# A larger GpSimd descriptor ring, setup weights on row buffers, and exponentials written back into their bank

## The reference

```python
h = _L0_tok_ref(x, ...)                              # embedding, hashed n-gram rows, scan, MLP
h = h + _L0_attn_ref(_layernorm(h, axis=-1), ...)    # windowed attention with shifted keys
h = h + _L0_ffn_ref(_layernorm(h, axis=-1), ...)     # 8 experts, the best one is taken
h = h + _L1_attn_ref(_layernorm(h, axis=-1), ...)    # "diagonal" attention, 8 heads
h = h + _L1_ffn_ref(_layernorm(h, axis=-1), ...)     # product keys, 16 table rows per head, causal attention
```

## Time and profile before

| what | value |
| --- | --- |
| median of 3 runs | 7602.68 us |
| lowest and highest | 7565.14 and 7603.8 us |
| the profiled execution | 7555.76 us |
| its span | 7554.0 us |
| mean granted TensorE clock | 0.655 of full speed |
| PE, DVE, ACT, POOL busy | 47%, 40%, 32%, 60% of the span |

### The profile page before, as it was taken

The page is one execution under the profiler, slowest core; times in us unless marked ns, Lnnn a source line. Parts: engine busy times, 40 slices in busy tenths (PEclk is TensorE's granted clock), DMA queues, the critical chain, the costliest instruction groups (busy, mean ns, idle before and its releaser), DMA issues.

```text
span 7554.0 us, 47644 instructions
## 1 busy us (share of the span) xinstructions
PE 3587.5 (47%) x10858; PEld 1925.2 (25%) x10858; DVE 2987.1 (40%) x10577; ACT 2449.4 (32%) x6449; POOL 4565.1 (60%) x4472
## 2 busy tenths in 40 slices
PE   3569979623334444443444345433543444444334
PEld 1247754211112212221222122211221222122112
DVE  4667744443333333332333333433433333333301
ACT  1247733212333333332333333322332323332222
POOL 4238820046666666666666666766666666666764
PEclk8567866556666666666666666766666666666667
DMA  1000012211112221122122111212121122111221
GB/s 24 13 17 24 23 37 79 71 36 51 49 48 50 54 50 48 49 54 49 47 48 56 47 49 49 55 48 49 48 55 48 48 49 49 48 45 46 48 46 31
DMA packets 228682, 346.51 MB, mean 46 GB/s; under 512 B 111343, under 2 KB 150836, under 8 KB 228416
## 3 DMA queue, kind: packets, MB, share of 16 engines
q0 software_dynamic: 135168, 272.90, 15.0%
q1 hardware_dynamic: 93248, 70.74, 3.0%
HBM read 310.84 MB, written 32.52 MB: 45 GB/s over the span
## 4 chain that ended last, share of the span: by engine, by line
another core or an unknown queue 28%; DVE 24%; issue 22%; PE 5%; ACT 2%; DVEq 0%; ACTq 0%
DVE sq_is_cand L2027 3%; PE sq_ps_v L1764 3%; DVE sq_is_cand L2025 3%; DVE sq_row_f L2029 3%; DVE sq_kv L2075 2%; DVE sq_d_negmax L1934 2%; DVE sq_top_at L1996 1%; ACT sq_rows L1892 1%; DVE sq_c_negmax L2080 1%; DVE sq_sim_rest L1984 1%; DVE sq_top_at L1985 1%; DVE sq_tops L1992 1%; DVE sq_cand_rest L1984 1%; DVE sq_tops L1980 1%
## 5 line engine op out<-in xcount | busy, mean ns | idle before, releaser
L1676 POOL DMA_INDIRECT sq_rows<-in_L_ffn_table,sq_row x4096 | 4005.9, 978 | 2082.2 <-issue 1218.1
L1764 PE MATMUL sq_ps_v<-sq_rows,sq_ident 128*128 128x512 f32 x2048 | 1360.3, 825 | 953.3 <-remote 412.0
L1892 ACT ACTIVATE sq_rows<-sq_rows,sq_weight 128x128 f32<-128x128 f32 x4096 | 1250.7, 397 | 207.3 <-issue 200.2
L1764 PEld LDWEIGHTS sq_ps_v<-sq_rows,sq_ident 128*128 128x128 f32 x2048 | 532.5, 274 | 1648.6 <-issue 802.6
L1843 ACT ACTIVATE sq_prob<-sq_ps_c,sq_c_negmax 128x128 f32<-128x128 f32 (+3 forms) x256 | 135.1, 528 | 1726.6 <-remote 630.6
L1832 ACT ACTIVATE sq_exp_out<-sq_ps_d,sq_d_negmax 128x512 f32<-128x512 f32 x256 | 175.7, 686 | 1574.9 <-DVE sq_d_negmax L1934 771.8
L2075 DVE TENSOR_REDUCE sq_kv<-sq_ps_v 128x128 f32<-128x512 f32 x256 | 175.8, 687 | 1023.9 <-remote 739.7
L1722 PE MATMUL sq_ps_c<-sq_kT,sq_qT 64*128 64x512 f32 (+3 forms) x512 | 256.7, 588 | 437.8 <-issue 238.8
L1708 PE MATMUL sq_ps_t<-sq_ident,sq_kv 128*128 128x128 f32 x128 | 35.2, 429 | 814.5 <-DVE sq_kv L2075 554.6
L1700 PE MATMUL sq_ps_d<-sq_d_q,sq_d_k 64*128 64x512 f32 x512 | 348.5, 781 | 133.8 <-ACT sq_exp_out L1832 108.9
L1730 PE MATMUL sq_ps_t<-sq_ident,sq_prob 128*128 128x128 f32 x640 | 147.6, 340 | 553.2 <-ACT sq_kT L1838 317.2
(11 more groups left out here) (333 smaller groups left out, 5706.1 us busy)
## 6 DMA issues: line engine op xcount, KB each, us to landing
sq_rows<-in_L_ffn_table,sq_row POOLq DMA_INDIRECT x4096
qkvT<-exp_rows SPq DMA_DIRECT2D x32, 768.0 KB, 3.3
sq_d_q<-qkvT SPq DMA_DIRECT2D x8, 1024.0 KB
sq_d_k<-qkvT SPq DMA_DIRECT2D x32, 256.0 KB
sq_d_v<-qkvT SPq DMA_DIRECT2D x32, 256.0 KB
at_parts_dram<-at_parts SPq DMA_DIRECT2D x8, 384.0 KB, 2.3
at_qS<-at_parts_dram SPq DMA_DIRECT2D x48, 64.0 KB, 2.3
at_kS<-at_parts_dram SPq DMA_DIRECT2D x48, 64.0 KB, 2.3
```

Source lines behind the costliest of these rows:

```text
L1676: pool.indirect_dma_start(rows[u % GSLOTS][:, k, :], None, w2["table"], bass.IndirectOffsetOnAxis(row[tile % 3][:, h, k:k + 1], 0)).then_i ...
L1764: mm = pe.matmul(ps_v[:, :], ident[:, :], slot[:, 4 * k:4 * k + 4, :].rearrange("p k c -> p (k c)"), start=(k == 0), stop=(k == TOPK // 4 ...
L1892: ins = act.activation(slot[:, k, :], slot[:, k, :], ACT.Copy, scale=weight[tile % 3][:, h, k:k + 1])
```

## The change

Three edits. The constructor gets `dynamic_dma_scratch_size=32768`. `exp_out`, 2 x 2 KB of a partition, is removed, and the exponentials are written into `ps_d`, from which they are read; the row sum goes where it went. `wpkT` and `keysT`, 4 KB of a partition each, become views of the first 32 partitions of row buffers 3 and 4, whose rows are 128 floats wide, so that each group of 64 floats takes the first half of one row. The row buffers are written by gathers only in the second block.

```diff
--- before.py
+++ after.py
@@ -1507,7 +1507,6 @@
         d_negmax, d_sums, d_attn = (sb("d_" + n, [P, UN]) for n in ("negmax", "sums", "attn"))
         d_prod = sb("d_prod", [P, PAIRS, P])
         head_sum = sb("head_sum", [P, 2])
-        exp_out = [sb(f"exp_out{k}", [P, T]) for k in R]
         weighted = sb("weighted", [P, HEADS1, D])
         mid = sb("mid", [P, 2 * TT, D])
 
@@ -1516,8 +1515,6 @@
         std = sb("std", [P, 1])
         xn = sb("xn", [P, D])
         xnT = sb("xnT", [D, TT, P])
-        wpkT = sb("wpkT", [DKEY, GROUPS, D])
-        keysT = sb("keysT", [DKEY, GROUPS, NKEYS])
         wsim = sb("wsim", [D, GROUPS * NKEYS])
         wq = sb("wq", [D, HEADS2 * D])
 
@@ -1540,6 +1537,8 @@
         weight = [sb(f"weight{b}", [P, HEADS2, TOPK]) for b in range(3)]
         wsum = sb("wsum", [P, HEADS2])
         rows = [sb(f"rows{k}", [P, TOPK, KV]) for k in range(GSLOTS)]
+
+        wpkT, keysT = rows[3][0:DKEY, :, 0:D], rows[4][0:DKEY, :, 0:NKEYS]
 
         qT = [sb(f"qT{b}", [P, PAIRS, T]) for b in R]
         kv = [sb(f"kv{b}", [P, TT, 2, HEADS2, D]) for b in R]
@@ -1829,7 +1828,7 @@
                     act.wait_ge(S["d_bias"], d + 1)
 
                     act.wait_ge(S["d_exp"], d + 1)
-                    act.activation(exp_out[d % 2][:, :], ps_d[d % 2][:, :], ACT.Exp, bias=d_negmax[:, d % UN:d % UN + 1],
+                    act.activation(ps_d[d % 2][:, :], ps_d[d % 2][:, :], ACT.Exp, bias=d_negmax[:, d % UN:d % UN + 1],
                                    accum_out=d_sums[:, d % UN:d % UN + 1]).then_inc(S["d_exp"], 1)
 
                 def keys(tile):
@@ -2158,7 +2157,7 @@
     t["L1_ffn_keysT"] = laid["L1_ffn_pk_keys"].transpose(3, 0, 2, 1).reshape(DKEY, GROUPS, NKEYS)
     t["L1_ffn_table"] = np.concatenate([laid["L1_ffn_keys_table"], laid["L1_ffn_values_table"]], axis=1)
     laid.update(t)
-    nc = bacc.Bacc("TRN2", target_bir_lowering=False, num_devices=1)
+    nc = bacc.Bacc("TRN2", target_bir_lowering=False, num_devices=1, dynamic_dma_scratch_size=32768)
     arrays, aps = {}, {}
     for name in LAID:
         v = np.ascontiguousarray(laid[name])
```

## The result

| what | before | after |
| --- | --- | --- |
| median of 20 runs each | 7580.04 us | 7614.16 us |
| lowest and highest | 7549.77 and 7603.80 | 7584.35 and 7638.94 |
| ratio after/before | | 1.0045, 95% interval 1.0033 to 1.0057 |
| the profiled execution | 7555.76 us | 7601.73 us |
| mean granted clock | 0.655 | 0.651 |

The change makes the kernel 34 us slower. That is small, but outside what scatter can make. The range of the prediction (7525 to 7650) holds the time; its likeliest case, no change, did not come true as it was argued: one term of its sum was set to 0 and is about +34 to +43 us.

The account below looks back on a forecast made before the run. It took GpSimd's gathers, waiting for late compute engines, to bound the main loop. -1.6 - 4 + 2 = -4 us, applied to the median of three runs (7602.7) and lowered a few us, gave 7595 us, range 7525 to 7650.

Parts of the forecast that it names:

- no change: Whole kernel: time stays within 0.5% (38 us) either way, as no ring wait shows in the loop; 65%.
- What bounds the kernel: Last stage's main loop: GpSimd waits 740 us ahead of units for buffers that slow compute engines free late.
- Part 1: Ring from 16 to 32 KB: -1.6 us in the first stage, 0 in the main loop, +20 as bad end.
- signs for this part: Ring right if the first stage's 1.89 us gap goes and gaps within a unit stay at 0.3 us.
- The sign for the whole: Main loop of the last stage: prediction wrong if its 5990 us change by over 38.
- The good side: First stage, 114th gather: a single 1.89 us wait for ring room goes, saving 1.59 us once.
- Part 2: Diagonal exponentials (L1832) kept in PSUM: 686 ns to 0.65 us each, 10 us of ScalarE time; -4 us taken.
- Rival C: Diagonal exponentials (L1832): ScalarE passes the bank twice, 0.43 us more each, half of 109 us on the path: 7655; 8%.
- Part 3: Last stage's setup: weights land on row buffers in 256-byte pieces, loads come 0 to 6 us later; +2 us taken.
- B: Main loop: a fifth of the 400 us of "remote" waits is for ring room, so -80 us, 7520; 7%.
- E: Gathers: each 0.02 us slower with the larger ring, +82 us, half given back, so +41: 7640; 4%.
- D: Main loop: slow stretches fall otherwise, waits ahead of units change by 50 us: 7650 or 7545; 10% faster, 5% slower.

Follow-up runs that it names:

- r16: The kernel after with the ring back at 16384 bytes, so the exponential and weight edits alone: 7570.81 us, ratio 1.0007 against before.
- b_r20: The kernel before with nothing changed but a ring of 20480 bytes: 7619.86 us, ratio 1.0061 against before.
- slots6: The kernel after with a ring of 16384 bytes and six row buffers instead of five: 7552.18 us, ratio 0.9974 against before.
- r8: The kernel after with a ring of 8192 bytes instead of 32768: 7572.53 us, ratio 1.0000 against before.
- r17: The kernel after with a ring of 17408 bytes instead of 32768: 7571.02 us, ratio 1.0003 against before.
- slots7: The kernel after with a ring of 16384 bytes and seven row buffers instead of five: 7560.57 us, ratio 0.9984 against before.
- ten16: The kernel after with a ring of 16384 bytes and ten gather semaphores instead of five: 7577.08 us, ratio 0.9997 against before.

## Why the prediction was wrong

**What bounds the kernel: right on the place, not on the reason.** GpSimd works against waits at the head of each unit, in the loop; the late starts are all at these heads, and edits that touch only other engines (r16, 1.0007) move nothing that can be told. But the prediction has the buffers freed late because the mix on TensorE is late, and the rows do not bear that out. TensorE ahead of the release at 3878.45 shown above, in the kernel after:

```profile
3844.17 5.18 PE L1763 MATMUL sq_ps_v<-sq_rows,sq_ident 128*128 128x512 f32 x8 [1.56 <-ACT sq_rows L1891]
...
3851.96 0.49 PE L1722 MATMUL sq_ps_c<-sq_future,sq_ident 128*128 128x128 f32 x2
3879.20 1.11 PE L1707 MATMUL sq_ps_t<-sq_ident,sq_kv 128*128 128x128 f32 x4 [26.75 <-DVE sq_kv L2074]
```

The mix's last matmul ended at 3849.35, later matmuls ended too, and TensorE then stood until the mix's semaphore rose at 3878.43, 29 us after the mix. Over the units that GpSimd waited for and whose increment is recorded, it came 18.3 us after the mix's last matmul in the median of 98 in the kernel before, and 19.7 us in that of 99 after; in 73 and 76 of them it was over 5 us. So most of GpSimd's waiting is for an increment that comes long after the work, in both kernels. What holds it back was not tried and stays open.

**Part 1: the failed step.** The step reads "as the cadence stayed at 1.25 us ... which excludes a cost that grows with the ring's fill, I take 0 and keep +20 as an end". The measured term is +34 us for the change and +38 for the ring alone (b_r20), well over the end of +20: the first gather of every fourth unit, when GpSimd had waited for it, started 0.99 or 1.60 us later, 53 us in direct sum. Three things went wrong. I looked for ring costs as gaps inside units, where the loops here show none over 0.32 us but the seven of slots6, and not in how late a unit's first gather starts after it is let go, though the earlier trace rows had this 0.24 us in it. I took the cadence as proof that the ring costs nothing, when it shows only that no cost comes to light in a run. And I asked whether a larger ring is dearer, not where its upkeep falls. With the old ring it would fall, by the theory, on the second gather of a unit and be covered, and the kernel before would be free of late starts by luck. That the 1.89 us of the earlier trace rows are a wait for room in a ring that 113 gathers have filled is not shown either: r8, with half the ring, has no such gap. The prediction's signs for this part misled as well: the 1.89 us of the earlier trace rows are gone and the gaps within a unit are still 0.3, both of which it had named as signs that the part was right. The sign for the whole, a loop that changes by over 38 us, was met by a hair (+39.5). The good side was right. The same gather, after and in r16:

```profile
286.65 0.94 POOL L346 DMA_INDIRECT tok_rows<-in_L_tok_hash_rows,tok_idx_now  x1 [0.30 <-issue]
```
```profile
285.90 0.95 POOL L346 DMA_INDIRECT tok_rows<-in_L_tok_hash_rows,tok_idx_now  x1 [2.01 <-issue]
```

**Part 2: right on the instruction.** The exponential takes 655 ns instead of 686, 128x512 in the loop (busy us, mean ns, idle before):

```profile
L1831 ACT ACTIVATE sq_ps_d<-sq_ps_d,sq_d_negmax 128x512 f32<-128x512 f32 x233 | 152.7, 655 | 1406.4 <-DVE sq_d_negmax L1933 610.2 <-remote 561.9 <-issue 233.6
L1842 ACT ACTIVATE sq_prob<-sq_ps_c,sq_c_negmax 128x512 f32<-128x512 f32 x56 | 38.3, 684 | 347.4 <-remote 161.6 <-issue 103.2 <-DVE sq_c_negmax L2079 82.5
```

L1842, which still writes to SBUF, stayed nearly where it was (684 against 687), so the 31 ns are the place of the result. 256 x 0.031 = 8 us of ScalarE time, and none of it in r16's time (1.0007): the 4 us that I took are below what can be told. Rival C is out.

**Part 3: no delay.** I had taken +2 us. The setup after (start us, us, engine, line, what), against the earlier trace rows:

```profile
1382.70 0.61 SPq L1588 DMA_DIRECT2D sq_rows<-in_L_ffn_keysT  x1
...
1385.59 1.96 PE L1623 MATMUL sq_ps_f<-sq_rows 32*64 32x64 f32 x16 [10.91 <-DMA sq_rows<-in_L_ffn_keysT]
...
1398.32 1.23 PE L1699 MATMUL sq_ps_d<-sq_d_q,sq_d_k 64*128 64x512 f32 x2 [8.03 <-ACT sq_d_q L1825]
```

From SP's issue of the second weight to TensorE's first use are 2.89 us; before 3.21 (1390.32 to 1393.53). To the first score matmul are 15.62 us; before 16.36 (1390.32 to 1406.68). The small pieces do not show.

**Rivals.** B fell: the waits named "remote" and PE did shrink, from 740.6 to 522.7 us, but "issue" grew by 278.8, so the waits ahead of units rose by 61 us in sum. E had the right sign and nearly the right size (+41 us) by a wrong mechanism, dearer gathers; the median gather is 944 ns. D, another fall of the slow stretches, is not needed: r16, r17 and r8 lay out SBUF anew too, and all three are within 0.1% of before. **The base.** I took the median of three runs, 7602.68; twenty give 7580.04. So the time fell near my number (7614 against 7595) partly by luck: a base some 20 us too high made up for more than half of the missing +34.

## What to carry to other kernels

In these kernels, what came with the size of the ring and the number of semaphores did not show in a run of gathers, but for seven gaps of 0.76 us in slots6, and cost 0.4 to 1.6 us on the first gather after a wait. Where either is changed (16192 bytes for 16384 cost 27 us here), ask on which gather such a cost could fall, and measure the time from the releasing semaphore to the start, not only the gaps between instructions. In the kernel after, all 40 of GpSimd's waits in the loop that are named "issue" and are over 0.4 us stand ahead of a first gather at a multiple of four, the 39 late starts and unit 8; the change of such names from one kernel to the next is worth following.

## What the runs showed of the hardware

- With some rings and semaphores the first gather of a unit after a wait starts late: by 0.99 us (1.60 at a tile's first unit, where the code has two waits in a row) when this can come once in 64 gathers, by 0.80 (1.23) for 48, by 0.43 (0.48) for 16. In a run of gathers at 1.25 us each nothing shows, but for the seven gaps of 0.76 us in slots6. That it is one and the same cost in both places is inferred.
- Without the argument for the ring the kernel before has the starts of r16, which gives 16384 (0.26 and 0.76 us), and the same gap before the 114th gather.
- A ring of 8192 bytes is as fast as one of 16384 here (1.0000 and 1.0007), and one of 20480 slower than both (1.0062); so is one of 16192 (1.0039).
- With 16384 bytes one gap of 1.89 to 2.02 us stands inside a run of the first stage, before the 114th gather of the program (r16 above, slots6, slots7 and ten16). With 8192, 16192, 17408, 20480 and 32768 bytes there is none. Why stays open.
- ScalarE took 31 ns less for the 128x512 exponential of the diagonal when it wrote into PSUM (655 ns in after) than when it wrote into SBUF (686 in before).
- The increment of the mix's semaphore came 18.3 us (before) and 19.7 us (after) behind the end of the mix's last matmul in the median of the units that GpSimd waited for.
- The slow stretches of the compute engines are there in every kernel run: of the 1024 maxima into `tops`, 98 to 127 start 1.1 to 1.3 us after VectorE's last instruction. Their link to GpSimd's gathers, which the prediction suspected, was not tried and stays open.
